# Weighted sweep of a graph network: second weights transposed in f32 from the landed cells, split into halves behind the transpose

## The chip, the cores and the metric

The kernel runs on one core of a Trainium2 chip. The metric is the device time of one execution in microseconds, as the median over runs. A profiled execution gives the trace from which rows are read.

## What is computed

Four graph layers run in turn over 3125 nodes of 256 features and 50000 edges, each followed by a residual and a layer norm. Only the first one carries the two edge weights that this case is about:

```python
a_in  = segment_sum(feat_in[src]  * iw[:, None], dst, num_segments=N)
a_out = segment_sum(feat_out[dst] * ow[:, None], src, num_segments=N)
```

`feat_in` and `feat_out` are two projections of the normalised features. The other layers use the plain edge counts between nodes.

## The kernel before

The sums over edges are products with dense 3125 x 3125 matrices. Earlier stages of the kernel scatter the edges into `cell_mat`, a matrix in HBM whose cells hold three f32 values side by side: the count of edges, the first weight (for `a_in`) and the second (for `a_out`).

The weighted sweep reads that matrix once. The 25 node tiles of 125 rows are grouped into 7 column ranges: six of 4 tiles (500 columns) and one of a single tile (125 columns). `IN_STEPS` lists 175 steps, range by range, 25 row tiles `t` in each. One step has a block of 125 rows by 500 cells, 1500 f32 values a row. It goes through these stages:

- SP loads the block into one of three `cells` buffers (L385, `load_cells(n + 3)` once step n has been split) and stores the counts of the step, which POOL has cast to f16 (L524), to `count_mat` (L390).
- ACT makes the f16 high half of both weights at once (L664: 1000 elements a partition, read from every third f32 value of a row). DVE makes the low half, value minus high half (L1407). `split[n % 3]` then holds two halves (`c`) of two weights (`q`).
- PE multiplies the first weight into `in_acc` with six f16 products of 500 columns (L944, in `in_part`) and adds the counts into `deg_acc` with one more (L947).
- PE transposes the second weight, half by half, with eight f16 transposes into the PSUM buffer `turn[n % 2]` (L955, in `turns`). ACT copies these 1000 values a partition to `outw` in SBUF (L655, in `turned`), which has a place for each of the 4 steps of a group and is a single buffer.
- After each group of 4 row tiles (the seventh group of a range has one tile), `out_part` multiplies the 4 transposed tiles into `out_acc` with 24 products (L930), and DVE adds the result to `aout` (L1387 in the first range, L1390 after it, in `added`).

The order on each engine is written out by hand. PE does `in_part(n)`, `turns(n)`, and then, in the first step of the next group, the `out_part` of the group that is complete (at the first step of a range `turns` and `out_part` stand ahead of `in_part`). ACT does the high half of step n, then `turned(n - 2)`; the first `turned` of a group waits until the `out_part` of the group before has read `outw`. DVE does the low half of step n, then, in the third step of a group, `added` for the group before, which waits for `out_part`. At the end of a range DVE also takes the degrees out of `deg_acc` (L1397 to L1399) and inverts them (L1401), and ACT copies `in_acc` out (L658); the first products of the next range wait for both.

Of the kernel before, what the change touches and what calls it, by code (L numbers as in the profile page):

```python
# [7 lines left out]
F16 = mybir.dt.float16  # L8
# [3 lines left out]
ALU = mybir.AluOpType  # L12
# [16 lines left out]
def build_gnn(nc, x, src, dst, edge_attr, edge_w, edge_w2, gamma0, beta0, W_in, b_in, W_out, b_out, W_x2i, b_x2i,  # L29
# [63 lines left out]
    with ExitStack() as ctx:  # L93
# [36 lines left out]
        q0 = 9 * COLS  # L130
        split = [Q[0:P, q0 + s * 2 * COLS:q0 + (s + 1) * 2 * COLS].bitcast(F16).rearrange("p (c q n) -> p c q n", c=2, q=2) for s in range(3)]
        q1 = q0 + 6 * COLS
        counts = [Q[:, q1 + s * COLS // 2:q1 + (s + 1) * COLS // 2].bitcast(F16) for s in range(4)]
# [122 lines left out]
        deg_acc = psum[:, 4, 0:COLS]  # L256
        turn = [psum[0:P, 5 + s, :].bitcast(F16).rearrange("p (k c n) -> p k c n", k=WIDE, c=2)[:, :, :, 0:P] for s in range(2)]

# [5 lines left out]
        def wide_slot(n, w):  # L264
# [6 lines left out]
                 "abs_done eq_done before_done claim_done free_ready w_ready sum_done ded_read vals_ready attr_hi attr_lo onehot_ready attr_done s_ready "  # L271
                 "hi_ready lo_ready count_ready step_done turned in_read deg_read out_mm out_added deg_staged "
                 "first_scale gates gate_used mv_ready std_ready norm_ready agr_ready agg_ready piece_used "
# [76 lines left out]
        def _(sp):  # L350
# [37 lines left out]
            for n, (r, t) in enumerate(IN_STEPS):  # L388
                sp.wait_ge(S["count_ready"], n + 1)
                sp.dma_start(count_block(r, t // ROWS)[:, t % ROWS], counts[n % 4][:, 0:RANGES[r][1] * P]).then_inc(count_stored[n % 4], 16)  # L390
                if n + 3 < NS:
                    sp.wait_ge(S["lo_ready"], n + 1)
                    load_cells(n + 3)
                if t == 2 and r:
                    q0_, qw = RANGES[r - 1][0] * P, RANGES[r - 1][1] * P
                    sp.wait_ge(S["deg_staged"], r)
                    sp.dma_start(deg_d[:, q0_:q0_ + qw], deg_stage[(r - 1) % 2][:, 0:qw]).then_inc(deg_kept[(r - 1) % 2], 16)
# [130 lines left out]
        def _(act):  # L528
# [119 lines left out]

            def turned(n):
                r, t = IN_STEPS[n]  # L650
                nt, tt = RANGES[r][1], t % WIDE
                act.wait_ge(S["step_done"], n + 1)
                if tt == 0 and n:
                    act.wait_ge(S["out_mm"], r * NR + t // WIDE)
                act.activation(outw[:, 0:nt, :, tt * P:(tt + 1) * P], turn[n % 2][:, 0:nt], ACT.Copy).then_inc(S["turned"], 1)  # L655
                if t == NT - 1:
                    c0, w = RANGES[r][0] * P, nt * P
                    act.activation(ain[:, :, c0:c0 + w], in_acc[:, :, 0:w], ACT.Copy, scale=unscale0).then_inc(S["in_read"], 1)  # L658
            for n, (r, t) in enumerate(IN_STEPS):
                w = RANGES[r][1] * P  # L660
                act.wait_ge(cells_in[n % 3], 16 * (n // 3 + 1))
                if n >= 3:
                    act.wait_ge(S["step_done"], n - 2)
                act.activation(split[n % 3][:, 0, :, 0:w], cells[n % 3][0:P, 0:3 * w].rearrange("p (n c) -> p c n", c=3)[:, 1:3],  # L664
                               ACT.Copy, scale=scale0[0:P, 1:2]).then_inc(S["hi_ready"], 1)
                if n >= 2:
                    turned(n - 2)
            for n in (NS - 2, NS - 1):
                turned(n)

# [130 lines left out]
        def _(pe):  # L801
# [132 lines left out]
            def in_part(n):  # L934
                r, t = IN_STEPS[n]
                w = RANGES[r][1] * P
                if t == 0:
                    if r:
                        pe.wait_ge(S["in_read"], r)
                        pe.wait_ge(S["deg_read"], r)  # L940
                for hh in range(2):
                    f = slice(hh * 128, (hh + 1) * 128)
                    for q, (c, d) in enumerate(((0, 0), (0, 1), (1, 0))):
                        pe.matmul(in_acc[:, hh, 0:w], feat[0][:, t, c, f], split[n % 3][:, d, 0, 0:w],  # L944
                                  start=t == 0 and q == 0, stop=t == NT - 1 and q == 2, skip_group_check=True)
                pe.wait_ge(S["count_ready"], n + 1)
                return pe.matmul(deg_acc[:, 0:w], ones16, counts[n % 4][0:P, 0:w], start=t == 0, stop=t == NT - 1, skip_group_check=True)  # L947

            def turns(n):
                r, t = IN_STEPS[n]  # L950
                if n >= 2:
                    pe.wait_ge(S["turned"], n - 1)
                for k in range(RANGES[r][1]):
                    for c in range(2):
                        last = pe.transpose(turn[n % 2][:, k, c], split[n % 3][:, c, 1, k * P:(k + 1) * P], ident16[0:P, 0:P])  # L955
                return last

            pe.wait_ge(S["s_ready"], 2)
            pe.wait_ge(S["feat_split"], 2 * PIECES)
            pending = None  # L960
            groups = 0
            for n, (r, t) in enumerate(IN_STEPS):
                pe.wait_ge(S["lo_ready"], n + 1)
                if t == 0:
                    turns(n)
                    if pending is not None:
                        out_part(pending)
                    in_part(n).then_inc(S["step_done"], 1)
                else:
                    in_part(n)  # L970
                    turns(n).then_inc(S["step_done"], 1)
                    if pending is not None:
                        out_part(pending)
                pending = None
                if t % WIDE == WIDE - 1 or t == NT - 1:
                    pending = groups
                    groups += 1
# [188 lines left out]
        def _(dve):  # L1166
# [225 lines left out]
            def degree(r, again):  # L1392
# [8 lines left out]
                link(dve.reciprocal(ROW[:, c0:c0 + w], ROW[:, c0:c0 + w]))  # L1401

            done = 0
            for n, (r, t) in enumerate(IN_STEPS):
                w = RANGES[r][1] * P
                dve.wait_ge(S["hi_ready"], n + 1)
                dve.scalar_tensor_tensor(out=split[n % 3][:, 1, :, 0:w], in0=cells[n % 3][0:P, 0:3 * w].rearrange("p (n c) -> p c n", c=3)[:, 1:3],  # L1407
                                         scalar=scale0[0:P, 1:2], in1=split[n % 3][:, 0, :, 0:w], op0=ALU.mult, op1=ALU.subtract).then_inc(S["lo_ready"], 1)
                if (t % WIDE == 2 and t > 2) or (t in (0, 2) and r):
                    added(done)  # L1410
                    done += 1
                if t == 0 and r:
                    dve.wait_ge(S["step_done"], n)
                    degree(r - 1, False)
            dve.wait_ge(S["step_done"], NS)
            degree(NR - 1, False)
# [212 lines left out]
```

## Time and profile before

| | |
|---|---|
| median of 3 runs | 3228.72 us (3227.2 to 3229.95) |
| profiled execution, its own time | 3224.97 us |
| span of its trace | 3223.1 us |
| TensorE (PE) busy in the span | 2547.6 us, 79% |
| VectorE (DVE) busy | 1684.7 us, 52% |
| ScalarE (ACT) busy | 1255.8 us, 39% |
| GpSimd (POOL) busy | 822.0 us, 26% |

The own time of the profiled execution lies 1.87 us above its span and 3.75 us below the median of the runs. Busy shares are means over stages with different limits; the weighted sweep is one stage of several.

### The profile page before, as it was taken

Reading aid. Unit: us, or ns where it says so; the run is one execution under the profiler, and the core shown is the slowest. Engines: PE = TensorE matmul, PEld = TensorE weight load, DVE = VectorE, ACT = ScalarE, POOL = GpSimd, SP = SyncE. Lnnn points to the kernel's source line nnn. Section 1 sums busy time; section 2 is a strip of 40 time slices with the busy share of each in tenths; the row PEclk is TensorE's granted clock in tenths of the full one; section 3 lists DMA queues with packets and bytes.
Section 4 is the critical chain, followed back from the end, with each engine's and each line's share of the span. In section 5 each row is a group of like instructions: output and inputs, shape, how many; then the busy total and the mean of one; then the engine's idle time right before and its main releaser. Section 6 shows DMA issues by size and latency. Waiting matters only on the chain.

```text
span 3223.1 us, 36451 instructions
## 1 busy us (share of the span) xinstructions
PE 2547.6 (79%) x14593; PEld 1397.2 (43%) x14593; DVE 1684.7 (52%) x1858; ACT 1255.8 (39%) x2535; POOL 822.0 (26%) x611
## 2 busy tenths in 40 slices
PE   0561047777777777889999799998999989999896
PEld 0320023333333333445444444555555665545543
DVE  3442579999999996555555545102122234132314
ACT  0138057677777613666666513001011121111203
POOL 3000467777777752223222200000000000000000
PEclk9795579999999999999999999999999999999897
DMA  9999853333333324777777543323323224333242
GB/s 371 405 386 409 269 110 49 59 58 59 59 59 53 44 17 153 236 245 245 247 237 242 144 124 75 124 72 106 105 81 96 96 78 127 109 111 105 84 148 67
DMA packets 220444, 472.29 MB, mean 147 GB/s; under 512 B 85174, under 2 KB 132942, under 8 KB 220044
## 3 DMA queue, kind: packets, MB, share of 16 engines
q1 hardware_dynamic: 140885, 426.39, 39.1%
q0 software_dynamic: 57360, 0.92, 4.9%
q10 hardware_dynamic: 22023, 42.59, 4.1%
q8 instruction: 117, 1.92, 0.2%
q14 instruction: 59, 0.48, 0.0%
HBM read 319.59 MB, written 150.22 MB: 146 GB/s over the span
## 4 chain that ended last, share of the span: by engine, by line
PE 48%; DMA 13%; POOL 11%; SPq 10%; DVE 8%; issue 6%; ACT 4%; ACTq 0%; DVEq 0%; POOLq 0%
PE psum L1050 25%; POOL cell_mat L515 11%; PE psum L998 11%; DMA cell_mat<-ROW 10%; SPq L356 10%; PE psum L930 6%; ACT Q L664 3%; DVE AR L1342 2%; DVE Q L1407 2%; PE psum L944 2%; DMA Q<-cell_mat 1%; PE psum L1067 1%; ACT Q L655 1%; DMA cell_mat<-SA 1%; PE psum L1077 1%
## 5 line engine op out<-in xcount | busy, mean ns | idle before, releaser
L1050 PE MATMUL psum<-FR 125*128 125x500 f16 (+1 forms) x4200 | 822.3, 355 | 20.8 <-DVE FR L1461 20.8
L515 POOL DMA_INDIRECT cell_mat<-ROW x391 | 622.9, 1593 | 534.7 <-DMA cell_mat<-SA 327.5
L900 PE MATMUL psum<-AR,Q 128*128 128x500 f16 (+1 forms) x2737 | 592.8, 356 | 183.7 <-DVE AR L1342 179.8
L1342 DVE TENSOR_SCALAR AR<-Q,ROW 128x3125 f16<-128x3125 f16 x391 | 721.2, 1900 | 7.0 <-PE psum L900 0.5
L1050 PEld LDWEIGHTS psum<-FR 125*128 125x128 f16 x4200 | 387.7, 98 | 428.9 <-issue 44.3
L900 PEld LDWEIGHTS psum<-AR,Q 128*128 128x128 f16 x2737 | 237.4, 98 | 455.2 <-DVE AR L1342 182.3
L1488 DVE SCALAR_TENSOR_TENSOR Q<-psum,small,ROW 128x1000 f32<-128x1000 f32 (+1 forms) x42 | 48.2, 1147 | 712.6 <-PE psum L1050 712.5
L1407 DVE SCALAR_TENSOR_TENSOR Q<-Q,small 125x1000 f16<-125x1000 f32 (+1 forms) x175 | 251.1, 1438 | 178.7 <-ACT Q L664 178.5
L524 POOL CAST Q<-Q 128x500 f16<-128x500 f32 (+1 forms) x175 | 173.8, 994 | 487.7 <-DMA Q<-cell_mat 472.2
L998 PE MATMUL psum<-wl,Q 128*125 128x256 f32 (+1 forms) x1100 | 286.8, 401 | 5.7 <-ACT Q L721 3.0
L944 PE MATMUL psum<-Q,FR 125*128 125x500 f16 (+1 forms) x1050 | 233.9, 360 | 60.2 <-DVE Q L1407 58.4
L664 ACT ACTIVATE Q<-Q,small 125x1000 f16<-125x1000 f32 (+1 forms) x175 | 261.9, 1497 | 35.7 <-DMA Q<-cell_mat 35.5
L597 ACT ACTIVATE AR<-AR,ROW 128x384 bf16<-128x384 f32 x391 | 235.0, 601 | 11.9 <-DMA AR<-cell_rows 11.5
L655 ACT ACTIVATE Q<-psum 125x1000 f16<-125x1000 f16 (+1 forms) x175 | 160.3, 916 | 166.4 <-PE psum L930 136.5
L998 PEld LDWEIGHTS psum<-wl,Q 128*125 128x125 f32 x1100 | 197.8, 188 | 62.3 <-issue 25.5
L930 PE MATMUL psum<-Q,FR 125*128 125x500 f16 (+1 forms) x1050 | 207.9, 353 | 9.2 <-DVE AR L1390 7.1
L605 ACT ACTIVATE AR<-AR 128x384 bf16<-128x384 bf16 x391 | 198.6, 508 | 0.0
L637 ACT ACTIVATE ROW<-psum 128x1 f32<-128x1 f32 x391 | 64.9, 166 | 297.5 <-PE psum L876 297.4
L709 ACT ACTIVATE Q<-psum 128x1000 f32<-128x1000 f32 (+1 forms) x35 | 32.0, 914 | 367.5 <-PE psum L1077 367.5
L944 PEld LDWEIGHTS psum<-Q,FR 125*128 125x128 f16 x1050 | 91.3, 100 | 153.2 <-DVE Q L1407 71.3
L930 PEld LDWEIGHTS psum<-Q,FR 125*128 125x128 f16 x1050 | 94.1, 97 | 104.9 <-ACT Q L655 8.4
L639 ACT ACTIVATE ROW<-SA,ROW 128x9 bf16<-128x9 bf16 x391 | 119.1, 305 | 12.6
(278 smaller groups left out, 2324.1 us busy)
## 6 DMA issues: line engine op xcount, KB each, us to landing
cell_mat<-SA SPq DMA_DIRECT2D x39, 3000.0 KB, 31.7
Q<-cell_mat SPq DMA_DIRECT2D x150, 750.0 KB, 5.3
FR<-count_mat SPq DMA_DIRECT2D x180, 625.0 KB, 3.8
AR<-cell_rows ACTq DMA_DIRECT2D x47, 640.0 KB, 4.2
count_mat<-Q SPq DMA_DIRECT2D x150, 125.0 KB, 4.9
AR<-in_edge_attr SPq DMA_DIRECT2D x13, 960.0 KB, 4.9
Q<-in_edge_attr SPq DMA_DIRECT2D x48, 256.0 KB, 4.3
cell_mat<-ROW POOLq DMA_INDIRECT x391, 3.1
```

The lines of the kernel that those rows point to most:

```text
L356: sp.dma_start(flat_cells[j * SLAB:(j + 1) * SLAB].rearrange("(p k a) -> p k a", p=128, k=REPEAT), zero_block.unsqueeze(1).to_broadcast([1 ...
L515: pool.indirect_dma_start(out=cell_mat, out_offset=bass.IndirectOffsetOnAxis(ap=at[c % VALS][:, k:k + 1], axis=0), in_=vals[c % VALS][:, k ...
L597: act.activation(apart[t % 2].rearrange("p (j n) -> p j n", j=3), rows[c % 2][:, k:k + 3], ACT.Abs, bias=cell_neg[:, t:t + 1]).then_inc(S[ ...
L605: act.activation(same[c % 3][:, k], apart[t % 2].rearrange("p (j n) -> p j n", j=3), ACT.Relu, bias=1.0, scale=-1.0).then_inc(S["eq_done"], 1)
L664: act.activation(split[n % 3][:, 0, :, 0:w], cells[n % 3][0:P, 0:3 * w].rearrange("p (n c) -> p c n", c=3)[:, 1:3], ACT.Copy, scale=scale0 ...
L900: last = pe.matmul(a, own_attr, onehot[t % 3][:, t0:t0 + nt], start=t == 0, stop=t == ET - 1, skip_group_check=True)
L930: last = pe.matmul(out_acc[:, hh, 0:ws], feat[1][:, t0 + k, c, f], outw[:, k, d, 0:ws], start=k == 0 and q == 0, stop=k == nt - 1 and q == ...
L944: pe.matmul(in_acc[:, hh, 0:w], feat[0][:, t, c, f], split[n % 3][:, d, 0, 0:w], start=t == 0 and q == 0, stop=t == NT - 1 and q == 2, ski ...
L998: last = pe.matmul(o, a[:, k * P:(k + 1) * P], wt, start=q == 0, stop=bias is None and q == len(ops) - 1)
L1050: last = pe.matmul(a[:, hh, 0:w], parts[:, c, t, f], slot(m, j)[0:P, i_, :], start=t == 0 and c == 0, stop=t == NT - 1 and c == 1, skip_gr ...
L1342: dve.tensor_scalar(onehot[t % 3], iota16, dst_c[:, t:t + 1], None, ALU.is_equal).then_inc(S["onehot_ready"], 1)
L1407: dve.scalar_tensor_tensor(out=split[n % 3][:, 1, :, 0:w], in0=cells[n % 3][0:P, 0:3 * w].rearrange("p (n c) -> p c n", c=3)[:, 1:3], scal ...
```

## The change

Only the first weight is still split ahead of the products: ACT and DVE now handle 500 elements a step there instead of 1000. The second weight is transposed as f32 straight from the `cells` buffer by four f32 transposes, whose input is every third f32 value of a row; `turn[n % 2]` now holds 500 f32 values a partition. Behind the transpose ACT makes the high half from PSUM into `outw` (`turned_hi`) and DVE the low half from PSUM and that high half (`turned_lo`).

The orders change with it. PE does `in_part(n)`, then `turns(n + 1)`, then a pending `out_part`, in every step. ACT does the high half of step n, then `turned_hi(n - 1)`; the copy of `in_acc` becomes `in_out(r)`, between the two in the first step of the next range. DVE does the low half of step n, then `turned_lo(n - 1)`, then `added` and the degrees where they are due. SP waits for `turns_done` as well before it loads into a buffer again.

```diff
-        split = [Q[0:P, q0 + s * 2 * COLS:...].bitcast(F16).rearrange("p (c q n) -> p c q n", c=2, q=2) for s in range(3)]
+        split = [Q[0:P, q0 + s * COLS:...].bitcast(F16).rearrange("p (c n) -> p c n", c=2) for s in range(3)]
-        turn = [psum[0:P, 5 + s, :].bitcast(F16).rearrange("p (k c n) -> p k c n", k=WIDE, c=2)[:, :, :, 0:P] for s in range(2)]
+        turn = [psum[0:P, 5 + s, 0:COLS].rearrange("p (k n) -> p k n", k=WIDE) for s in range(2)]
...
# SP
                     sp.wait_ge(S["lo_ready"], n + 1)
+                    sp.wait_ge(S["turns_done"], n + 1)
                     load_cells(n + 3)
...
# ACT
-            def turned(n):
+            def turned_hi(n):
                 r, t = IN_STEPS[n]
                 nt, tt = RANGES[r][1], t % WIDE
-                act.wait_ge(S["step_done"], n + 1)
+                act.wait_ge(S["turns_done"], n + 1)
                 if tt == 0 and n:
                     act.wait_ge(S["out_mm"], r * NR + t // WIDE)
-                act.activation(outw[:, 0:nt, :, tt * P:(tt + 1) * P], turn[n % 2][:, 0:nt], ACT.Copy).then_inc(S["turned"], 1)
-                if t == NT - 1:
-                    c0, w = RANGES[r][0] * P, nt * P
-                    act.activation(ain[:, :, c0:c0 + w], in_acc[:, :, 0:w], ACT.Copy, scale=unscale0).then_inc(S["in_read"], 1)
+                act.activation(outw[:, 0:nt, 0, tt * P:(tt + 1) * P], turn[n % 2][:, 0:nt], ACT.Copy, scale=scale0[0:P, 1:2]).then_inc(S["turn_hi"], 1)
+
+            def in_out(r):
+                c0, w = RANGES[r][0] * P, RANGES[r][1] * P
+                act.wait_ge(S["step_done"], (r + 1) * NT)
+                act.activation(ain[:, :, c0:c0 + w], in_acc[:, :, 0:w], ACT.Copy, scale=unscale0).then_inc(S["in_read"], 1)
...
-                act.activation(split[n % 3][:, 0, :, 0:w], cells[n % 3][0:P, 0:3 * w].rearrange("p (n c) -> p c n", c=3)[:, 1:3],
+                act.activation(split[n % 3][:, 0, 0:w], cells[n % 3][0:P, 0:3 * w].rearrange("p (n c) -> p n c", c=3)[:, :, 1],
                                ACT.Copy, scale=scale0[0:P, 1:2]).then_inc(S["hi_ready"], 1)
-                if n >= 2:
-                    turned(n - 2)
-            for n in (NS - 2, NS - 1):
-                turned(n)
+                if t == 0 and r:
+                    in_out(r - 1)
+                if n:
+                    turned_hi(n - 1)
+            turned_hi(NS - 1)
+            in_out(NR - 1)
...
# PE
             def turns(n):
                 r, t = IN_STEPS[n]
+                pe.wait_ge(cells_in[n % 3], 16 * (n // 3 + 1))
                 if n >= 2:
                     pe.wait_ge(S["turned"], n - 1)
                 for k in range(RANGES[r][1]):
-                    for c in range(2):
-                        last = pe.transpose(turn[n % 2][:, k, c], split[n % 3][:, c, 1, k * P:(k + 1) * P], ident16[0:P, 0:P])
-                return last
+                    last = pe.transpose(turn[n % 2][:, k], cells[n % 3][0:P, 0:3 * COLS].rearrange("p (n c) -> p n c", c=3)[:, k * P:(k + 1) * P, 2], ident[0:P, 0:P])
+                last.then_inc(S["turns_done"], 1)
...
+            turns(0)
             for n, (r, t) in enumerate(IN_STEPS):
                 pe.wait_ge(S["lo_ready"], n + 1)
-                if t == 0:
-                    turns(n)
-                    if pending is not None:
-                        out_part(pending)
-                    in_part(n).then_inc(S["step_done"], 1)
-                else:
-                    in_part(n)
-                    turns(n).then_inc(S["step_done"], 1)
-                    if pending is not None:
-                        out_part(pending)
+                in_part(n).then_inc(S["step_done"], 1)
+                if n + 1 < NS:
+                    turns(n + 1)
+                if pending is not None:
+                    out_part(pending)
...
# DVE
+            def turned_lo(n):
+                r, t = IN_STEPS[n]
+                nt, now = RANGES[r][1], slice(t % WIDE * P, (t % WIDE + 1) * P)
+                dve.wait_ge(S["turn_hi"], n + 1)
+                dve.scalar_tensor_tensor(out=outw[:, 0:nt, 1, now], in0=turn[n % 2][:, 0:nt], scalar=scale0[0:P, 1:2], in1=outw[:, 0:nt, 0, now],
+                                         op0=ALU.mult, op1=ALU.subtract).then_inc(S["turned"], 1)
...
-                dve.scalar_tensor_tensor(out=split[n % 3][:, 1, :, 0:w], in0=cells[n % 3][0:P, 0:3 * w].rearrange("p (n c) -> p c n", c=3)[:, 1:3],
-                                         scalar=scale0[0:P, 1:2], in1=split[n % 3][:, 0, :, 0:w], op0=ALU.mult, op1=ALU.subtract).then_inc(S["lo_ready"], 1)
+                dve.scalar_tensor_tensor(out=split[n % 3][:, 1, 0:w], in0=cells[n % 3][0:P, 0:3 * w].rearrange("p (n c) -> p n c", c=3)[:, :, 1],
+                                         scalar=scale0[0:P, 1:2], in1=split[n % 3][:, 0, 0:w], op0=ALU.mult, op1=ALU.subtract).then_inc(S["lo_ready"], 1)
+                if n:
+                    turned_lo(n - 1)
                 if (t % WIDE == 2 and t > 2) or (t in (0, 2) and r):
                     added(done)
...
+            turned_lo(NS - 1)
```

## Rows read from the trace of the kernel before

**Rows 1.** The page's chain that ended last, shares of the span by line.

```profile
PE psum L1050 25%; POOL cell_mat L515 11%; PE psum L998 11%; DMA cell_mat<-ROW 10%; SPq L356 10%; PE psum L930 6%; ACT Q L664 3%; DVE AR L1342 2%; DVE Q L1407 2%; PE psum L944 2%; DMA Q<-cell_mat 1%; PE psum L1067 1%; ACT Q L655 1%; DMA cell_mat<-SA 1%; PE psum L1077 1%
```

**Rows 2.** Line L944: ns min/median/max, first and last start in us, forms.

```profile
L944 PE MATMUL psum<-Q,FR x1050: 215/374/627, 1252.9 to 1846.3; 125*128 125x500 f16 x150, 125*128 125x125 f16 x25
```

**Rows 3.** Chain in order of time over one group of four steps: start us, us, what.

```profile
1372.12 5.09 PE psum L930 x24
...
1377.30 0.04 ACT Q L655
...
1379.73 1.00 ACT Q L655
1380.73 1.53 ACT Q L664
...
1382.28 1.59 DVE Q L1407
...
1383.92 1.44 PE psum L944 x6
1385.36 0.21 PE psum L947
1385.57 0.46 PE psum L955 x8
1386.03 5.09 PE psum L930 x24
```

**Rows 4.** Timeline, the same group: start us, us, instruction, idle before and its releaser.

```profile
1381.49 1.44 PE L944 MATMUL psum<-Q,FR 125*128 125x500 f16 x6 [0.42 <-DVE Q L1407]
```

**Rows 5.** Groups by line and shape, whole sweep: busy us, mean ns, idle before.

```profile
L664 ACT ACTIVATE Q<-Q,small 125x1000 f16<-125x1000 f32 x150 | 246.0, 1640 | 27.9 <-DMA Q<-cell_mat 27.9
L1407 DVE SCALAR_TENSOR_TENSOR Q<-Q,small 125x1000 f16<-125x1000 f32 x150 | 237.4, 1586 | 166.4 <-ACT Q L664 166.3
...
L1390 DVE SCALAR_TENSOR_TENSOR AR<-psum,small,AR 128x1000 f32<-128x1000 f32 x36 | 45.3, 1258 | 77.3 <-PE psum L930 77.2
...
L664 ACT ACTIVATE Q<-Q,small 125x250 f16<-125x250 f32 x25 | 15.9, 634 | 7.8 <-DMA Q<-cell_mat 7.7
L1407 DVE SCALAR_TENSOR_TENSOR Q<-Q,small 125x250 f16<-125x250 f32 x25 | 13.7, 552 | 12.3 <-ACT Q L664 12.2
...
L658 ACT ACTIVATE AR<-psum,small 128x1000 f32<-128x1000 f32 x6 | 6.5, 1084 | 0.0
...
L1390 DVE SCALAR_TENSOR_TENSOR AR<-psum,small,AR 128x250 f32<-128x250 f32 x6 | 2.8, 473 | 0.7 <-PE psum L930 0.7
...
L658 ACT ACTIVATE AR<-psum,small 128x250 f32<-128x250 f32 x1 | 0.5, 464 | 0.0
```

**Rows 6.** Groups of ACT by line and shape, whole span: contiguous f32 to f16.

```profile
L620 ACT ACTIVATE Q<-Q,small 128x512 f16<-128x512 f32 x48 | 34.0, 708 | 56.3 <-PE psum L900 45.8 <-DMA Q<-in_edge_attr 10.5
L691 ACT ACTIVATE FR<-AR,small 125x1280 f16<-125x1280 f32 x25 | 31.9, 1349 | 17.6 <-DVE small L1554 11.2 <-issue 6.4
```

**Rows 7.** Chain in order of time around eight f32 transposes of a later stage.

```profile
2022.52 0.85 PE psum L1077 x8
```

**Rows 8.** Timeline at the end of the first range, DVE and PE.

```profile
1340.48 1.26 DVE L1387 TENSOR_SCALAR AR<-psum,small 128x1000 f32<-128x1000 f32 x1 [4.86 <-PE psum L930]
...
1341.66 0.66 DVE L1397 COPY gate<-psum 1x500 f32<-1x500 f32 x1
...
1343.52 3.28 DVE L1401 RECIPROCAL ROW<-ROW 128x500 f32<-128x500 f32 x1
...
1343.63 1.43 PE L944 MATMUL psum<-Q,FR 125*128 125x500 f16 x6 [0.26 <-DVE ROW L1399]
...
1348.43 1.44 PE L944 MATMUL psum<-Q,FR 125*128 125x500 f16 x6 [3.16 <-DVE Q L1407]
```

**Rows 9.** Windows at the end of the fourth range: PE busy, granted clock, DMA share, GB/s.

```profile
1630.00:1634.00 4.00, 4.00 (x18) 0.53 0.94 325
```

**Rows 10.** Loads and stores of tile Q, 1372 to 1400 us.

```profile
DMA to landing us min/median/max: 4.1/5.4/6.1
```

More of the change, by code:

```diff
@@ L130, in build_gnn @@
         q0 = 9 * COLS
-        split = [Q[0:P, q0 + s * 2 * COLS:q0 + (s + 1) * 2 * COLS].bitcast(F16).rearrange("p (c q n) -> p c q n", c=2, q=2) for s in range(3)]
-        q1 = q0 + 6 * COLS
+        split = [Q[0:P, q0 + s * COLS:q0 + (s + 1) * COLS].bitcast(F16).rearrange("p (c n) -> p c n", c=2) for s in range(3)]
+        q1 = q0 + 3 * COLS
         counts = [Q[:, q1 + s * COLS // 2:q1 + (s + 1) * COLS // 2].bitcast(F16) for s in range(4)]
@@ L271, in build_gnn @@
                  "abs_done eq_done before_done claim_done free_ready w_ready sum_done ded_read vals_ready attr_hi attr_lo onehot_ready attr_done s_ready "
-                 "hi_ready lo_ready count_ready step_done turned in_read deg_read out_mm out_added deg_staged "
+                 "hi_ready lo_ready count_ready step_done turns_done turn_hi turned in_read deg_read out_mm out_added deg_staged "
                  "first_scale gates gate_used mv_ready std_ready norm_ready agr_ready agg_ready piece_used "
@@ L943, in in_part @@
                     for q, (c, d) in enumerate(((0, 0), (0, 1), (1, 0))):
-                        pe.matmul(in_acc[:, hh, 0:w], feat[0][:, t, c, f], split[n % 3][:, d, 0, 0:w],
+                        pe.matmul(in_acc[:, hh, 0:w], feat[0][:, t, c, f], split[n % 3][:, d, 0:w],
                                   start=t == 0 and q == 0, stop=t == NT - 1 and q == 2, skip_group_check=True)
```

## The prediction

> **What bounds the kernel now.** I read the page's chain first: the lines of the weighted sweep (L930, L944, L664, L1407, L655) hold some 14% of the span there [rows 1]. From the first product of the sweep at 1252.9 us to the last step at 1846.3 us it takes about 594 us [rows 2]. All the rest of the kernel is untouched.
>
> Then the chain inside one group of four steps [rows 3]. The reader should see a period: the 24 products of an `out_part` end 13.91 us after the previous ones (1372.12 to 1386.03). PE alone would need less. The 24 products take 5.09, so one product of 500 columns takes 0.212 and the seven of a step 1.48; eight f16 transposes take 0.46; four steps and an `out_part` are 4 x 1.94 + 5.09 = 12.85. The missing microsecond is two waits for the low half, before the third and the fourth step after an `out_part` (the first of them stands as 0.42 us idle [rows 4]). They come from ACT: `outw` is a single buffer, so ACT stands still until `out_part` ends (1377.21), starts its copy 0.09 later, and then needs 1.00 + 1.53 us for copy and high half, and again for the next step; DVE adds 1.59 behind the last one [rows 3]. The third step's products start 4.28 us after the end of `out_part` (1381.49), those of the fourth 2.43 later. So PE has a small margin and ACT's pace sets the rest. When PE starts from a standstill, its 7 products end 1.65 us later (1.44 + 0.21), 0.17 more than their pitch; I add that after a wait.
>
> There are 30 such periods (five in each of the six wide ranges) and six range ends.
>
> **The parts and their prices.** First the halves at 500 elements, interpolated between 250 and 1000 [rows 5]. High half on ACT: 0.634 + (1.640 - 0.634)/3 = 0.97 (0.86 on the chain, as 1.53 stands there for 1.64). Low half on DVE: 0.552 + 1.034/3 = 0.90. `turned_hi`, priced as ACT's scaled copy from PSUM: 0.464 + 0.620/3 = 0.67. `turned_lo`, as DVE's `added`, also f32 from PSUM with a second operand: 0.473 + 0.785/3 = 0.735. ACT drops from 1.00 + 1.53 to about 1.53 a step on the chain; DVE has about the same work as before, but in two instructions, the second of which waits for PE and ACT.
>
> The transposes: eight f16 ones took 0.46, that is 0.0575 each [rows 3]; eight f32 ones with a contiguous input take 0.85, or 0.106 each [rows 7], so four cost 0.43, nearly the same. The new input is not contiguous: it takes every third f32 value. No row shows PE reading that way. The nearest rows are those of ACT and DVE on the same buffer with the same step: from 250 to 1000 elements they rise by 1.34 and 1.38 ns an element [rows 5], while ACT on contiguous f32 rises by (1349 - 708)/768 = 0.83 [rows 6]. Two engines with different rates of their own meet at one value, so I read it as a limit of such reads. If it holds for PE's weight load, 125 columns take 0.17 us; the load of one transpose overlaps the one before it, so the pitch becomes 0.17 and four cost 0.68. Bounds: 0.106 (the step costs nothing), and 0.34 (the f32 values are read twice). I take 0.17, the value of the nearest rows.
>
> The Trainium skill has a rule on this: "SBUF — State Buffer", section "Door 1: The DMA port swizzle", says that f32 can be read at steps of up to four values at full rate. By it the pitch would stay at 0.106 and the time would be that of the second rival below. The trace does not agree with it at a step of three [rows 5, 6].
>
> Now the new chain after an `out_part`. ACT still waits for its end before `turned_hi` of a group's first step, and behind that wait is queued the next high half. Behind `turned_lo`'s wait on DVE are queued `added` and the next low half; before the change `added` ran at once, under ACT's copy and high half, and cost nothing. That cover is gone: the order is now low half, `turned_lo`, `added`, low half. Start of ACT 0.09; `turned_hi` 0.67; high half 0.86; to DVE 0.02; low half 0.90 (second step: its products start 2.59 after the end of `out_part`); `turned_lo` 0.735; `added` 1.26 [rows 5]; low half of the third step 0.90; to PE 0.05; less 3 x 0.08, since DVE's instructions in a row overlap by that (1340.48 + 1.26 against 1341.66 [rows 8]): 5.24 us, against 4.28 before. PE is earlier: first step 1.48 + 0.68, then from 2.59 on 1.65 + 0.68 = 4.92. After the wait: 1.65 + 0.68, the fourth step 1.48 + 0.68 without a wait (its low half is ready near 6.7), and 5.09. Period: 5.24 + 2.33 + 2.16 + 5.09 = 14.82, **0.91 more** than 13.91. Times 30: 27.3 us.
>
> At a range end the products of the next range wait for `deg_read`. Before: 3.15 us after the end of `out_part` (1340.48 to 1343.63), and the step after that at 7.95 (1348.43), behind the reciprocal of 3.28 [rows 8]. Now `turned_hi` and `turned_lo` stand ahead of `added` and the three degree instructions: 0.09 + 0.67 + 0.02 + 0.735 + 1.26 + 3 x 0.66 - 4 x 0.08 + 0.05 = 4.49; the reciprocal and a low half of 0.90 put the next step at about 8.5 (PE's work between fits: 1.65 + 0.68 + a quarter of 5.09). That is 0.6 later, six times: 3.6 us. The idle stretch there grows to 4.4 us. Already now, after 3.16 us idle, the granted clock falls to half at four of the six ends; the window of the worst shows 0.53 with PE busy throughout, a loss of 4 x 0.47 = 1.9 us [rows 9]. I expect it at all six: 3.8 us.
>
> At nothing: SP's added wait (the transposes of a step end before its low half: 2.16 against 2.54 in the second step; only load and count store are behind it); the loads, unchanged in size; the last, narrow range, which loses and gains the same instructions at a quarter of the width (plus or minus 3 us). PE's new wait for the cells is hidden barely: the transposes just ahead of `out_part` start at 5.24 + 1.65 + 0.68 + 1.48 = 9.05, their cells were asked for at 2.54 and land 5.4 later, 6.1 at most [rows 10]: 0.4 to 1.1 us of cover.
>
> Sum: 27.3 + 3.6 + 3.8 = 34.7. Against the profiled execution's own 3224.97 that is 3259.7; the median of the runs is 3.75 above it, so **3263 us**.
>
> **The rivals.**
> - *The step of three costs PE nothing* (pitch 0.106). Period 5.24 + 1.65 + 0.43 + 1.91 + 5.09 = 14.32, 0.41 more: 12.3 + 3.6 + 3.8 = 19.7, so 3248. For it: the 0.85 of the contiguous f32 transposes; against it: the rise on two engines.
> - *The values are read twice* (0.34). PE alone then needs 4 x (1.48 + 1.36) + 5.09 = 16.45, 2.54 more: 76, and at a range end up to 4 x 0.9 = 3.6 more, 22 for six; with the clock 102, so 3331. Against it: nothing in the rows splits the load in two.
> - *Cells come late*: beyond 6.5 us of landing each microsecond costs one per group; 0.6 us would be 18 more, 3281.
> - *DVE keeps up, and the change is faster.* If the chain from `out_part` to the third step's low half were under 4.83 us at a pitch of 0.106, the period would fall below 13.91; with no such wait left PE sets it: 4 x 1.91 + 0.17 + 5.09 = 12.9, 1.0 less, 30 us for 30 periods; with 7.4 at the range ends 3206. For it: none of the four new durations was measured at 500 elements, and ACT has 1.0 us a step more to spare. Against it: 1.26 of `added` stand in program order and the durations lie between measured ones.
> - *No change*: the chain about 0.3 us shorter than I add up, at 0.106.
>
> **Numbers.** Chances: forecast 0.48, free step 0.24, read twice 0.12, late cells 0.05, faster 0.05, no change 0.06. A measurement of this kernel tells about 0.2%, 6.5 us, from nothing. The range reaches from the free step with its chain shortened by 0.5 us (3233) over the late cells to a pitch between 0.17 and 0.34 (3305); outside remain the double read and the faster cases, some 2 in 10. All but a few hundredths of the free-step case is slower by over 0.2%: faster 0.06, same 0.11, slower 0.83.
>
> **What the new profile should show.** Four f32 transposes at a pitch of 0.17; L1407's successor near 0.90, `turned_hi` 0.67, `turned_lo` 0.735; the third step's products waiting for the low half, DVE running `added` just ahead of it; a period near 14.8; 4.4 us of PE idle at each range end, released by DVE's degrees, and a halved clock behind it. A period below 13.9 or a third step that waits for nothing would make me wrong; a pitch of the transposes near 0.11 would make the size wrong.

## The result

| | median of the runs | runs |
|---|---|---|
| before | 3229.34 us | 4, 3227.2 to 3230.78 |
| after | 3263.82 us | 4, 3259.59 to 3264.64 |

The ratio is 1.0105, with an interval of 1.0087 to 1.0122: the change makes the kernel 1% slower. The profiled execution after took 3263.47 us, 38.5 more than that of before (3224.97).

### The profile page after: what moved, and what is told of

Read it like the earlier page. It is cut to its first block, busy times and chain, and to the rows that moved or that the text cites. A ratio compares the mean times of both kernels' runs of the same rounds, so it can differ in the third digit from the quotient of the medians.

```text
span 3261.7 us, 35715 instructions
## 1 busy us (share of the span) xinstructions
PE 2594.1 (80%) x13968; PEld 1431.6 (44%) x13968; DVE 1681.1 (52%) x2033; ACT 1105.2 (34%) x2535; POOL 787.5 (24%) x611
## 3 DMA queue, kind: packets, MB, share of 16 engines
q1 hardware_dynamic: 140885, 426.39, 38.5%
## 4 chain that ended last, share of the span: by engine, by line
PE 51%; DMA 12%; POOL 11%; SPq 10%; DVE 9%; issue 5%; ACT 2%; ACTq 0%; DVEq 0%; POOLq 0%
PE psum L1051 24%; DMA cell_mat<-ROW 11%; POOL cell_mat L516 11%; PE psum L999 11%; SPq L356 10%; PE psum L935 6%; PE psum L949 4%; DVE AR L1343 2%; PE psum L960 2%; DVE Q L1415 2%; DVE AR L1391 1%; ACT Q L667 1%; PE psum L1068 1%; DVE Q L1408 1%; DMA cell_mat<-SA 1%
## 5 line engine op out<-in xcount | busy, mean ns | idle before, releaser
L949 PE MATMUL psum<-Q,FR 125*128 125x500 f16 (+1 forms) x1050 | 236.7, 363 | 48.9 <-DVE ROW L1400 27.6
L525 POOL CAST Q<-Q 128x500 f16<-128x500 f32 (+1 forms) x175 | 138.4, 791 | 551.8 <-DMA Q<-cell_mat 541.6
L1408 DVE SCALAR_TENSOR_TENSOR Q<-psum,small,Q 125x500 f16<-125x500 f32 (+1 forms) x175 | 118.5, 677 | 255.6 <-ACT Q L656 255.6
L935 PE MATMUL psum<-Q,FR 125*128 125x500 f16 (+1 forms) x1050 | 214.5, 362 | 3.8 <-DVE AR L1391 3.8
L656 ACT ACTIVATE Q<-psum,small 125x500 f16<-125x500 f32 (+1 forms) x175 | 110.4, 631 | 309.4 <-PE psum L935 288.2
L667 ACT ACTIVATE Q<-Q,small 125x500 f16<-125x500 f32 (+1 forms) x175 | 157.2, 898 | 70.6 <-DMA Q<-cell_mat 69.1
L1415 DVE SCALAR_TENSOR_TENSOR Q<-Q,small 125x500 f16<-125x500 f32 (+1 forms) x175 | 148.2, 847 | 54.5 <-ACT Q L667 50.3
L949 PEld LDWEIGHTS psum<-Q,FR 125*128 125x128 f16 x1050 | 95.8, 102 | 147.7 <-issue 37.4
L960 PEld LDWEIGHTS psum<-ident,Q 125*125 125x125 f32 x625 | 126.8, 257 | 49.6 <-issue 36.0
```

The lines of the kernel that those rows point to most:

```text
L935: last = pe.matmul(out_acc[:, hh, 0:ws], feat[1][:, t0 + k, c, f], outw[:, k, d, 0:ws], start=k == 0 and q == 0, stop=k == nt - 1 and q == ...
L960: last = pe.transpose(turn[n % 2][:, k], cells[n % 3][0:P, 0:3 * COLS].rearrange("p (n c) -> p n c", c=3)[:, k * P:(k + 1) * P, 2], ident[ ...
L1415: dve.scalar_tensor_tensor(out=split[n % 3][:, 1, 0:w], in0=cells[n % 3][0:P, 0:3 * w].rearrange("p (n c) -> p n c", c=3)[:, :, 1], scalar ...
```

## The profile after

Line numbers move: `turned_hi` is L656 (ACT), the high half L667 (ACT), the low half L1415 (DVE), `turned_lo` L1408 (DVE), `added` L1388 and L1391 (DVE), the degrees L1398 to L1402 (DVE), the seven products of a step L949 and L952, the transposes L960, the products of an `out_part` L935 (all PE), the cast of the counts L525 (POOL).

First the groups by line and shape over the whole sweep (busy us, mean ns of one, idle before).

```profile
L667 ACT ACTIVATE Q<-Q,small 125x500 f16<-125x500 f32 x150 | 145.7, 971 | 63.0 <-DMA Q<-cell_mat 61.7 <-PE psum L952 1.3
L1415 DVE SCALAR_TENSOR_TENSOR Q<-Q,small 125x500 f16<-125x500 f32 x150 | 138.4, 923 | 50.3 <-ACT Q L667 46.1
L960 PE MATMUL psum<-ident,Q 125*125 125x125 f32 x625 | 134.3, 334 | 17.5 <-DVE Q L1408 10.9 <-DMA Q<-cell_mat 6.5
...
L1408 DVE SCALAR_TENSOR_TENSOR Q<-psum,small,Q 125x500 f16<-125x500 f32 x150 | 110.0, 733 | 239.9 <-ACT Q L656 239.9
...
L656 ACT ACTIVATE Q<-psum,small 125x500 f16<-125x500 f32 x150 | 101.3, 676 | 285.9 <-PE psum L935 264.9 <-PE psum L960 21.0
```

The four new prices were 0.97, 0.90, 0.735 and 0.67 us in the prediction; 0.971, 0.923, 0.733 and 0.676 are here. Reading 250 and 1000 elements off [rows 5] and going a third of the way between gave each to within 3%. The 334 ns of a transpose is not its pitch (the time from one start to the next), since the transposes of a step overlap; the pitch is read from the starts.

The chain in order of time over one group (start us, us, what), to be held against [rows 3]:

```profile
1376.76 5.09 PE psum L935 x24
...
1381.93 0.04 ACT Q L656
...
1382.50 0.97 ACT Q L667
...
1383.49 0.60 DVE Q L1415
...
1384.31 0.74 DVE Q L1408
1385.05 1.17 DVE AR L1391
1386.21 0.80 DVE Q L1415
...
1387.06 1.44 PE psum L949 x6
...
1390.81 0.62 PE psum L960 x4
1391.43 5.09 PE psum L935 x24
```

The chain leaves PE where `out_part` ends (1381.84), passes ACT (`turned_hi`, high half) and then stays on DVE: low half, `turned_lo`, `added`, low half, in that order of program. PE comes back with the third step at 1387.06, 5.22 us after `out_part` (4.28 in [rows 3]). From there PE alone sets the rest: two steps, then `out_part`. The period is 14.67. Four transposes take 0.62, a mean of 0.154 each, which the expectations below call their pitch. Their starts are not evenly spread. The last transposes on the timeline ahead of that `out_part`, one by one (PEld is PE's weight load):

```profile
1390.44 0.25 PEld L960 LDWEIGHTS psum<-ident,Q 125*125 125x125 f32 x1
1390.65 0.27 PE L960 MATMUL psum<-ident,Q 125*125 125x125 f32 x1
1390.75 0.33 PE L960 MATMUL psum<-ident,Q 125*125 125x125 f32 x1
1390.92 0.34 PE L960 MATMUL psum<-ident,Q 125*125 125x125 f32 x1
1391.09 0.33 PE L960 MATMUL psum<-ident,Q 125*125 125x125 f32 x1
```

The second transpose comes 0.106 behind the first, and the third, the fourth and the next product (1391.26) 0.17 each behind the one before; over the sweep the medians are 0.106 and 0.170. So a strided transpose does cost 0.17, but the first of a set does not pay it: its weight load starts together with the last product of the step (1390.44), whose 0.21 us are longer than 0.17. A set costs 0.106 + 3 x 0.17 = 0.62.

The waits of PE in the sweep (us in all, times, longest):

```profile
PE psum L949 <- DVE ROW L1400: 27.6, 6, 4.6
PE psum L949 <- DVE Q L1415: 20.8, 54, 1.1
PE psum L960 <- DVE Q L1408: 10.9, 41, 0.6
PE psum L960 <- DMA Q<-cell_mat: 6.5, 1, 6.5
PE psum L935 <- DVE AR L1391: 3.8, 1, 3.8
```

The first row is the range ends: six waits of about 4.6 us. The fourth says that PE waited for cells once, ahead of the first step. The last is the end of the sweep, where the last products wait for `added`. The end of the first range, DVE and PE, on the timeline (start us, us, instruction, idle before and its releaser), answers to [rows 8]:

```profile
1344.03 0.74 DVE L1408 SCALAR_TENSOR_TENSOR Q<-psum,small,Q 125x500 f16<-125x500 f32 x1 [6.41 <-ACT Q L656]
...
1344.68 1.25 DVE L1388 TENSOR_SCALAR AR<-psum,small 128x1000 f32<-128x1000 f32 x1
1345.85 0.66 DVE L1398 COPY gate<-psum 1x500 f32<-1x500 f32 x1
...
1347.02 0.66 DVE L1400 TENSOR_SCALAR ROW<-psum 128x500 f32<-128x500 f32 x1
...
1347.82 2.66 PE L949 MATMUL psum<-Q,FR 125*128 125x500 f16 x6 [4.61 <-DVE ROW L1400]
```

DVE had stood still for 6.41 us, behind its wait for `turned_hi`, while the degrees were ready to be read. The six products then take 2.66 us where they take 1.43 in [rows 8]: the clock is at half. The window behind the third range end (PE busy, PEld, DVE, ACT, POOL, granted clock, DMA share, GB/s):

```profile
1543.00:1547.00 4.00, 2.85 (x7) 1.22 (x8) 3.96 (x3) 0.00 (x0) 0.00 (x0) 0.50 0.00 0
```

0.50 is 1.2 GHz. The other five ends show 0.50 to 0.69 in such a window: the clock fell at all six.

Split by the starts of the full-width `out_part`s on the timelines of both kernels, the 38.6 us between the two spans (3223.1 and 3261.7) are:

| stretch | before | after | difference | predicted |
|---|---|---|---|---|
| start of the kernel to the first `out_part` | 1265.7 | 1264.0 | -1.6 | 0 |
| 30 periods | 418.5 | 443.9 | +25.4 | +27.3 |
| five range ends | 117.1 | 121.7 | +4.7 | +6.2 (5/6 of 3.6 + 3.8) |
| last full `out_part` to the end of the sweep | 49.0 | 58.5 | +9.5 | +1.2, plus or minus 3 |
| all after it | 1372.8 | 1373.5 | +0.6 | 0 |

The last stretch (the sixth end and the narrow range) is where the prediction was off. One group of the narrow range in the chain of before, and one in the chain of after:

```profile
1826.51 1.25 DVE AR L1390
...
1828.24 2.48 DMA Q<-cell_mat
```

```profile
1869.47 0.38 ACT Q L656
...
1869.87 0.35 DVE Q L1408
...
1870.85 1.17 DVE AR L1391
...
1874.06 2.51 PE psum L935 x6
```

Before, each group waited there for a transfer (2.48), and everything else fitted beside it. After, the chain is that of the wide ranges, from the end of `out_part` through ACT and DVE, and `added` in it is not a quarter of its size: it still takes 1.17, since its size goes by the row tiles of the group, four here too, and not by the width of the range (of the 36 at 1000 elements in [rows 5], six are those of the narrow range). The five periods between the six larger `out_part`s of the narrow range take 33.6 instead of 28.2, 5.3 more; their six products took 2.51 in this one and 1.28 where the clock was high. The mean clock was 0.83 from 1830 to 1890, against 0.93 from 1803 to 1852 before. The tail, from the last of those `out_part`s on, is 3.5 longer: the degrees again stand behind a `turned_lo` that waits for `out_part`, and `added` and the last products behind the degrees.

## The experiments

The theory: the third step waits for a chain that has become longer because DVE's `turned_lo` and `added` now stand ahead of the low half, all of it started by ACT's wait for the single `outw`; the strided transposes lengthen PE's part; the range ends lose because the degrees stand behind `turned_lo`. The main rival: the strided read of PE is the whole loss. Another: the read costs nothing, and the chain is all of it. A third: the cells land too late. Runs e1 to e4 share one set of runs of the kernel before (median 3229.36, 13 runs), e5 to e8 another (3228.73, 9 runs).

### e1: transposes from contiguous values

```diff
-last = pe.transpose(turn[n % 2][:, k], cells[n % 3][0:P, 0:3 * COLS].rearrange("p (n c) -> p n c", c=3)[:, k * P:(k + 1) * P, 2], ident[0:P, 0:P])
+last = pe.transpose(turn[n % 2][:, k], cells[n % 3][0:P, k * P:(k + 1) * P], ident[0:P, 0:P])
```

> The changed kernel, but its f32 transposes read 125 contiguous values of the landed block instead of every third one (so the second weights are the wrong cells; all amounts of work stay). Theory 1 (chain through DVE after each out_part, with the strided read a second, smaller term): the pitch of the transposes falls from 0.154 to 0.106 us; the third step still starts 5.2 us after out_part, and only the two sets of transposes behind it come earlier, so the period of a group falls by 2 x 0.19 = 0.38 to about 14.3, 30 times, and a little at the six range ends: about 3249 us, 15 less than the changed kernel. Theory 2 (the strided read is the whole cost of the change): back to about 3229. Theory 3 (neither, the cells land too late): no change from 3264.

Measured: 3249.84 us, 1.0066 of before (1.0049 to 1.0083), 14 less than after. The chain:

```profile
1388.26 0.43 PE psum L960 x4
```

Four transposes take 0.43, a mean of 0.107, that of [rows 7]. Two steps of four transposes follow the third step's wait, so a period loses 8 x (0.154 - 0.107) = 0.37; the usual period is 14.29 instead of 14.67. The mean falls by 0.30, from 14.80 to 14.50, which is 9 us; the five range ends give 4 and the last stretch 2. The step of three costs 14 of the 34.5 us; without it the kernel is still 20 slower than before. None of the three rivals stands.

### e5 and e6: steps of two and four

```diff
-cells[n % 3][0:P, 0:3 * COLS].rearrange("p (n c) -> p n c", c=3)[:, k * P:(k + 1) * P, 2]
+cells[n % 3][0:P, 0:2 * COLS].rearrange("p (n c) -> p n c", c=2)[:, k * P:(k + 1) * P, 1]
```

In e6 the same place reads:

```diff
+cells[n % 3][0:P, 0:4 * P].rearrange("p (n c) -> p n c", c=4)[:, :, k]
```

> The changed kernel, but the f32 transposes read every second value of the landed block (wrong cells, same amounts of work). If PE's weight load pays for each 16 bytes that a read of single values runs over, a step of 8 bytes still finds two values in 16 bytes and the pitch of the transposes stays near the contiguous 0.107 us; if it pays in proportion to the step, the pitch is halfway to 0.154, about 0.13.

> The changed kernel, but the f32 transposes read every fourth value (16 bytes apart; wrong cells, same amounts of work). If single values in different 16 bytes are what costs, every value now stands alone and the pitch rises above the 0.154 us of the step of three, to about 0.2; if any step above one costs the same, it stays 0.154.

Measured, one run each: 3250.12 and 3274.99 us. From the chains, e5 first:

```profile
1388.14 0.46 PE psum L960 x4
```

```profile
1379.84 0.81 PE psum L960 x4
```

So four transposes at steps of one, two, three and four values take 0.43, 0.46, 0.62 and 0.81 us. On the timelines the median time between the starts behind the first two of a set is 0.109, 0.116, 0.170 and 0.229. The gap ahead of them is 0.106 at steps up to three and 0.121 at four, where a load of 0.229 is longer than the product of 0.21 ahead of it; both fit a first load that runs under that product.

125 values at a step of three lie in 1500 bytes, which are 94 pieces of 16 bytes; at a step of four each lies in a piece of its own, 125. Per piece that is 0.170/94 = 1.81 ns and 0.229/125 = 1.83; at a step of two it would be 63 x 1.82 = 0.115, against 0.116 measured, and for contiguous values 0.06, below the 0.109 that they take anyway. ACT and DVE, at a step of three, rise by 1.34 and 1.38 ns an element [rows 5], which is 1.79 and 1.84 for each 16 bytes: one rate on three engines. The numbers fit a cost by the bytes run over, and not by the value. Whether a piece of 16 bytes is the unit is not shown: at these steps pieces of 16 bytes or of more and the mere length all give the same times, and no run has a step above four.

In e6 the period is 15.06 us: 8 x 0.0485 = 0.39 more than 14.67.

### e2: `added` one step later

```diff
-                if (t % WIDE == 2 and t > 2) or (t in (0, 2) and r):
+                if (t % WIDE == 3 and t > 3) or (t in (0, 2) and r):
```

> The changed kernel, but DVE does added one step later, behind the low halves that the third step waits for. Theory 1: the low half of the third step is ready about 4.0 us after out_part, so PE goes from the second step to the third without a wait (4.9 instead of 5.2), and nothing else of DVE's stands in the way of the rest: the period falls from 14.67 to about 14.2, 30 times 0.5: about 3249 us. Theory 2 (strided read alone): no change from 3264. Theory 3 (cells too late): no change.

Measured: 3247.82 us, 1.0061 of before (1.0045 to 1.0078), 16 less than after. The chain:

```profile
1380.53 0.96 ACT Q L667
1381.52 1.28 DVE Q L1415
...
1382.84 1.44 PE psum L949 x6
...
1385.11 1.27 PE psum L949 x6
```

PE now waits ahead of the second step only (1382.84) and goes on to the third (1385.11) and fourth without a wait. The mean period is 14.35 instead of 14.80: 30 x 0.45 = 13.4, and the last stretch falls from 58.5 to 54.0. With `added` out of its way the second step still comes 2.97 us after the end of `out_part` (1379.87 to 1382.84), by the chain that starts at ACT's wait. That is a period with a long low half (1.28); in the usual ones, of 14.15, it comes after 2.60, where the prediction had 2.59.

### e3: the degrees ahead of `turned_lo` and `added`

```diff
+                if t == 0 and r:
+                    dve.wait_ge(S["step_done"], n)
+                    degree(r - 1, False)
                 if n:
                     turned_lo(n - 1)
                 if (t % WIDE == 2 and t > 2) or (t in (0, 2) and r):
                     added(done)
                     done += 1
-                if t == 0 and r:
-                    dve.wait_ge(S["step_done"], n)
-                    degree(r - 1, False)
```

> The changed kernel, but at a range end DVE takes the degrees out ahead of turned_lo and added, while the last full out_part still runs. Theory 1: the wait of 4.6 us for deg_read at the six range ends goes, and with it most of the stretches at half clock behind them: 6 x (4.6 + 1.5 to 2) = 37 to 40 us less, about 3226 us. Rival: the range end is bound by the loads of the next cells, which take the place of that wait: under 12 us less, 3252 or more.

Measured: 3230.03 us (10 runs), 1.0005 of before (0.9996 to 1.0015), 34 less than after. The timeline at the end of the first range:

```profile
1337.18 0.67 DVE L1398 COPY gate<-psum 1x500 f32<-1x500 f32 x1
...
1339.05 3.28 DVE L1402 RECIPROCAL ROW<-ROW 128x500 f32<-128x500 f32 x1
```

```profile
1337.60 5.24 PE L935 MATMUL psum<-Q,FR 125*128 125x500 f16 x24
1342.67 1.43 PE L949 MATMUL psum<-Q,FR 125*128 125x500 f16 x6
```

The degrees and the reciprocal lie under the 5.24 us of `out_part`, where DVE had nothing to do; PE goes on at once, at full clock. The five range ends take 92.8 us instead of 121.7 and the last stretch 52.7 instead of 58.5, while the 30 periods stay at 14.81: the two losses are separate. The move gives back far more than the 4.7 us that the five ends had lost by the change, so most of what it removes was there before the change; e8 asks how much.

### e8: the same move in the kernel before

```diff
+                if t == 0 and r:
+                    dve.wait_ge(S["step_done"], n)
+                    degree(r - 1, False)
                 if (t % WIDE == 2 and t > 2) or (t in (0, 2) and r):
                     added(done)
                     done += 1
-                if t == 0 and r:
-                    dve.wait_ge(S["step_done"], n)
-                    degree(r - 1, False)
```

> The kernel before the change, with the degrees taken out early at a range end and nothing else. Theory 1: there the reciprocal (3.28 us) stood ahead of the low half that the second step of a range waits for 3.2 us; without it that step starts 2.7 us earlier, six times, and the half-clock stretches behind go: 16 to 22 us less, about 3210 us; the wait for deg_read itself was only 0.26 us there. Rival: no change, since the halves of the next steps wait for ACT anyway.

Measured: 3200.65 us (4 runs), 0.9915 (0.99 to 0.9931), 28 less than before. The expected size was too small: the five ends fall from 117.1 to 94.5 (22.5), and the sixth, in the last stretch, by 5.2, that is 4.6 an end where 2.7 and the half clock had been counted (up to 3.7). With the degrees early in both kernels the change costs 3230.03 - 3200.65 = 29 us (the two runs stand beside different sets of before, 0.6 apart); the periods give 26 of it (444.4 against 418.1) and the last stretch 9, while the start and the five ends are 5 shorter.

### e4: two `outw` buffers

The smaller split frees room: the tiles of the sweep in `Q` end at column 9000 instead of 10500, of 11000, so that a second `outw` of 2000 fits, which it did not before.

```diff
-        outw = Q[0:P, q2:q2 + 4 * COLS].bitcast(F16).rearrange("p (k c n) -> p k c n", k=WIDE, c=2)
+        outw2 = [Q[0:P, q2 + s * 4 * COLS:q2 + (s + 1) * 4 * COLS].bitcast(F16).rearrange("p (k c n) -> p k c n", k=WIDE, c=2) for s in range(2)]
...
-                if tt == 0 and n:
-                    act.wait_ge(S["out_mm"], r * NR + t // WIDE)
+                gi = r * NR + t // WIDE
+                outw = outw2[gi % 2]
+                if tt == 0 and gi >= 2:
+                    act.wait_ge(S["out_mm"], gi - 1)
```

DVE's `turned_lo` and the products of `out_part` take the buffer of their group in the same way.

> The changed kernel with two outw buffers (in the space that the smaller split gave free), so that turned_hi of a new group need not wait for the out_part of the one before. Theory 1: ACT and DVE then work through out_part, PE finds the halves of all four steps ready, and the period falls to PE's own 4 x (1.48 + 0.62) + 5.09 = 13.5 us from 14.67 to 14.8: 30 x 1.2 = 36 us less, about 3228 us; the waits at the range ends stay. Theory 2 (only the transposes' pitch counts): no change, since the pitch stays 0.154. Theory 3 (cells land too late): the period stays above 14.3, with PE waiting for the loads, since the steps then come at 2.1 us each with three cell buffers: 3250 or more.

Measured: 3201.27 us, 0.9913 (0.9897 to 0.993), 62.5 less than after. The chain between two `out_part`s is PE alone (transposes L963, products L952 and L955):

```profile
1378.88 5.08 PE psum L938 x24
...
1385.43 0.62 PE psum L963 x4
...
1392.34 5.07 PE psum L938 x24
```

The period is 13.46, less than the 13.91 of [rows 3] although the transposes are dearer than before. I had expected 36 from the periods alone; 30 x (14.80 - 13.46) is 40, the five ends give 13 (21.7 each instead of 24.3), and the last stretch about 10. The wait for the degrees is still there (19.1 us in six waits).

### e7: two `outw` buffers and early degrees

The edits of e4 and e3 together.

> Two outw buffers and the degrees taken out early, together, on the changed kernel. Theory 1: the period stays at PE's own 13.46 us, and the wait of 3.2 us for deg_read at six range ends goes with the half clock behind it: 20 to 28 us less than the 3201 of two outw buffers alone, 3173 to 3181 us, faster than both kernels. Rival: with PE that fast the loads of the cells set the range ends, and less than 8 us is left of it: 3193 or more.

Measured: 3175.03 us (5 runs), 0.9832 (0.9818 to 0.9845): 26 less than e4, 89 less than after, 25.6 less than e8. The waits of PE from 1246 to 1890 us, all of them; L1002 belongs to the stage behind the sweep:

```profile
PE psum L963 <- DMA Q<-cell_mat: 9.1, 4, 6.6
PE psum L1002 <- DMA Q<-hT_d: 8.8, 1, 8.8
PE psum L952 <- DVE Q L1419: 6.0, 11, 1.1
PE psum L938 <- DVE AR L1394: 2.4, 3, 1.5
PE psum L963 <- DVE Q L1412: 0.5, 1, 0.5
```

The row for the degrees is gone. This version beats both kernels.

## Why the prediction was right

- **The period.** Forecast 14.82, a mean of 14.80 measured. It came right by the chain that was named: the third step starts 5.22 us after `out_part`, forecast 5.24, with `added` just ahead of its low half. e2 shows the part of `added` (the wait leaves the third step) and e4 the part of the single `outw` (all waits of the period go). That the mean fits to 0.02 is partly luck, since two smaller errors cancel in it: with every piece at its usual size the period is 14.67, because four transposes take 0.62 and not 0.68; but fourteen of the 30 come out at 14.8 to 15.2, because the low half of the second step is longer there. In the one shown in the last section (15.03) it took 1.27 and not 0.90, and 14.67 + 0.37 is that period.
- **The transposes.** The step of three costs PE, as forecast, and the pitch of 0.17 is what the starts show (0.170). Reading the rate of ACT and DVE as that of PE was a guess from far rows, and it held: 1.79, 1.84 and 1.82 ns for each 16 bytes. The mis-sized term is the set: "four cost 0.68" counts the first load too, which runs under the product ahead of it, so that four cost 0.62. The finer steps of e5 and e6 show that the unit is not the value. The Trainium skill, "SBUF — State Buffer", "Door 1: The DMA port swizzle", gives lines of 16 bytes and wants two reads in each for full rate, and concludes that f32 may be read at steps of up to four. The pitches do not agree with that conclusion (0.170 at three and 0.229 at four, against 0.109 for contiguous values and 0.116 at two), though they can be had from lines of 16 bytes; the measurement decides.
- **The range ends.** The 4.4 us of PE idle that were forecast measured 4.61, and the clock fell at all six ends. Five ends cost 4.7 instead of 6.2. e3 shows the cause: with the degrees earlier the wait and the half clock both go.
- **The narrow range.** "Plus or minus 3 us" for instructions "at a quarter of the width" was the worst mis-sized term: `added` keeps its full width there, and the stretch went from waiting for transfers to waiting for DVE. With the sixth end it cost 9.5 instead of 1.2. That the total fits so closely is luck: this made up for the periods and the ends, each a little cheaper than forecast (1.9 and 1.5), and for the earlier start (1.6). Against the profiled execution alone the forecast was 3259.7, 3.8 below the 3263.47 measured; the 3.75 that I added for the median was not needed after, whose median lies 0.35 above its profiled execution.
- **The rivals.** *Free step*: e1 makes it true and gives 3250, where 3248 was forecast; with the step of three it is false. *Read twice*: a pitch of 0.34 is excluded. *Late cells*: one wait for cells, at the start. *DVE keeps up*: the chain would have had to be below 4.83; it is 5.22. *No change*: the chain is 0.02 shorter than added up, not 0.3. What could make this split of the work faster was a different edit, e4's second buffer. The sentence on the Trainium skill calls the free step the second rival; it is the first of the list.

## What to carry to other kernels

When work moves to an engine that runs in program order, look at what it used to do for nothing in the stretch where it will now wait: `added` cost nothing until an instruction that waits for ACT stood in front of it, and the degrees, which already cost something (e8), cost more. Work that depends on nothing late (the degrees here) belongs ahead of the first waiting instruction, under a long stretch of products, and moving it is worth trying even in the old kernel (28 us). And when a change makes a buffer smaller, ask what single buffer could now be two: the room freed here was worth more (62 us) than the change had cost.

## What the runs showed of the hardware

- PE's weight load of f32 values at a step of two to four goes by the bytes run over, some 1.82 ns for each 16 (0.116, 0.170 and 0.229 us for 125 values), and a step of two is nearly free (contiguous: 0.109). ACT and DVE show the same rate at a step of three. No run tells the 16-byte piece from the mere length.
- The low half, whose two inputs both lie in SBUF, and a cast of POOL shut each other out: which of them begins first decides who waits. On the timeline of after, the 117 low halves with no cast beside them take 0.86 to 0.91 us. Of the 33 that overlap one, 27 begin after the cast; where the cast has over 0.3 us to go, they end 0.63 to 0.66 us behind its end. One such pair:

```profile
1397.94 0.85 POOL L525 CAST Q<-Q 128x500 f16<-128x500 f32 x1 [1.28 <-DMA Q<-cell_mat]
...
1398.16 1.27 DVE L1415 SCALAR_TENSOR_TENSOR Q<-Q,small 125x500 f16<-125x500 f32 x1
```

  Five of the six low halves that begin first stay at 0.87 to 0.90, and two casts beside them take 1.23 and 1.46 instead of 0.85; in the sixth the cast begins 6 ns behind it, and the low half takes 1.52. In the kernel before, the low half began first in 75 of 85 overlaps, and the cast, which is not on the chain of [rows 3], took the delay, ending 0.7 us behind the low half:

```profile
1407.69 1.56 DVE L1407 SCALAR_TENSOR_TENSOR Q<-Q,small 125x1000 f16<-125x1000 f32 x1 [1.38 <-ACT Q L664]
1408.63 1.31 POOL L524 CAST Q<-Q 128x500 f16<-128x500 f32 x1 [1.35 <-DMA Q<-cell_mat]
```

  After, the stretched low half of the second step lies on the chain: each period is 14.67 plus that stretch to within 0.02 us (all but the last, of 14.15), which makes 4 us in 30 periods. `turned_lo`, which reads one input from PSUM, overlaps the cast 62 times and stays at 0.72 to 0.76. The Trainium skill, "SBUF — State Buffer", "SBUF: two separate sides", has DVE with two SBUF inputs and GpSimd compete for one pair of ports, which the one that starts first holds for its whole instruction; the trace agrees, with the numbers above. No run took the cast away, so the cause is read from the order of the starts alone.
